# Moving two layer normalisations and a residual add into the loop of a feed-forward on one Trainium2 core

## What is computed

```python
x = x + layernorm(differential_attention(layernorm(x)))      # stage a
x = x + layernorm(depth_2_block(layernorm(x)))                # stages n0, b0, f0, b1, f1, n1
x = x + layernorm(state_space(layernorm(x)))                  # stage s
x = x + layernorm(mixture_of_experts(layernorm(x)))           # stage mx

# depth_2_block, twice (l = 0, 1): local attention (stage b), then the feed-forward (stage f)
h = shift_token(x)                       # the upper 64 features come from the token before
h = (h - mean) / sqrt(var + 1e-5) * ln_g + ln_b
a, g = split(h @ w1 + b1)                # 128 -> 2 x 341
x = x + (a * gelu(g)) @ w2 + b2          # 341 -> 128
```

## Time and profile before

| | us |
|---|---|
| median of 3 runs (2048.04 to 2049.25) | 2048.75 |
| profiled execution | 2051.13 |
| its span, first to last instruction | 2049.3 |
| PE busy in the span | 1719.8 |
| DVE busy | 1544.9 |
| ACT busy | 1363.4 |
| POOL busy | 877.9 |
| second feed-forward, from its first transposes to the last residual add | 1608.9 to 1690.6 |
| separate stage, from its first statistics to its last application | 1691.9 to 1725.8 |
| state space, from its first transposes | from 1726.0 |

### The profile page before, as it was taken

One profiled execution on the slowest core, in us unless ns is written; L12 is line 12 of the kernel. 1 busy time (PEld: TensorE's weight loads), 2 busy tenths in 40 slices (PEclk: granted clock), 3 DMA queues, 4 the chain that ended last, 5 costly groups with the idle time before them and its releaser, 6 DMA issues. The chain is left out here.

```text
span 2049.3 us, 39274 instructions
## 1 busy us (share of the span) xinstructions
PE 1719.8 (84%) x12410; PEld 1128.4 (55%) x12410; DVE 1544.9 (75%) x4156; ACT 1363.4 (67%) x4708; POOL 877.9 (43%) x816
## 2 busy tenths in 40 slices
PE   4999999999999955999999695999999683753991
PEld 2555555555555532777777352777777351552660
DVE  2898889988889965899999365899998365663445
ACT  2888888888888862888888222888888226322555
POOL 3555655555655543233233123233233123285555
PEclk9999999999999976999999896999999896755995
DMA  7990000000000000000000100000000100012324
GB/s 205 185 184 11 2 1 2 1 2 1 2 2 2 2 1 6 12 17 12 16 17 12 32 19 6 11 17 13 16 16 13 32 19 1 6 45 66 84 64 133
DMA packets 102525, 65.90 MB, mean 32 GB/s; under 512 B 27698, under 2 KB 93874, under 8 KB 102322
## 3 DMA queue, kind: packets, MB, share of 16 engines
q1 hardware_dynamic: 97970, 54.40, 13.3%
q0 software_dynamic: 4352, 8.99, 1.3%
HBM read 19.50 MB, written 30.24 MB: 24 GB/s over the span
## 5 line engine op out<-in xcount | busy, mean ns | idle before, releaser
L411 ACT ACTIVATE a_E<-a_psS,a_nm 128x128 f32<-128x128 f32 (+1 forms) x1028 | 419.9, 429 | 32.2 <-DVE a_nm L245 30.2
L216 POOL TENSOR_SCALAR a_aT<-a_dT 128x384 f32<-128x384 f32 x256 | 309.1, 1208 | 299.8 <-PE a_psO L529 187.6
L245 DVE TENSOR_REDUCE a_nm<-a_psS 128x2 f32<-128x256 f32 (+1 forms) x514 | 259.9, 546 | 43.9 <-PE a_psS L496 43.4
L492 PE MATMUL a_psS<-a_kT,a_qm 32*128 32x128 f32 (+1 forms) x2064 | 240.6, 351 | 5.4 <-issue 3.4
L270 DVE SCALAR_TENSOR_TENSOR a_d<-a_E,a_cf 128x128 f32<-128x128 f32 (+1 forms) x512 | 219.4, 468 | 27.9 <-DVE a_cf L259 1.4
L411 ACT ACTIVATION_READ_ACCUMULATOR a_E<-a_psS,a_nm 128x1 f32 x1028 | 220.7, 215 | 0.0
L830 POOL TENSOR_TENSOR b0rn<-b0ss,minus_half 128x16 f32<-128x16 f32 x36 | 107.2, 2977 | 223.6 <-DVE b0ss L866 223.6
L830 POOL TENSOR_TENSOR b1rn<-b1ss,minus_half 128x16 f32<-128x16 f32 x36 | 107.2, 2977 | 223.0 <-DVE b1ss L866 223.0
L420 ACT ACTIVATE a_dT<-a_psT 128x384 f32<-128x384 f32 x256 | 127.0, 496 | 73.9 <-PE a_psT L505 71.2
L492 PEld LDWEIGHTS a_psS<-a_kT,a_qm 32*128 32x128 f32 x2064 | 136.6, 186 | 55.9 <-issue 35.6
L505 PE MATMUL a_psT<-ident,a_d 128*128 128x128 f32 x768 | 132.6, 282 | 6.8 <-DVE a_d L270 1.0
(11 more groups left out here) (353 smaller groups left out, 4424.1 us busy)
## 6 DMA issues: line engine op xcount, KB each, us to landing
mx_rows<-mx_blank SPq DMA_DIRECT2D x9, 2080.0 KB, 31.2
mx_xin<-mx_rows SPq DMA_DIRECT2D x72, 65.0 KB
b0v<-b0v SPq DMA_DIRECT2D x34, 128.0 KB, 2.3
b1v<-b1v SPq DMA_DIRECT2D x34, 128.0 KB
F<-mx_results SPq DMA_DIRECT2D x8, 256.0 KB, 5.2
mx_second<-mx_results SPq DMA_DIRECT2D x8, 256.0 KB, 5.4
out_dram<-X SPq DMA_DIRECT2D x8, 256.0 KB, 2.3
f0z<-F SPq DMA_DIRECT2D x9, 128.0 KB
```

The source lines that it names most:

```text
L216: pool.tensor_scalar(aT[:, s, :], dT[:, s, :], 0.0, None, ALU.max).then_inc(positived.sem, 1)
L245: ins = dve.tensor_reduce(nm[:, s, t, :], psS[:, s, :, (0, P)[t]:(P, 384)[t]], axis=AX.X, op=ALU.max, negate=True)
L411: ins = act.activation(E[:, s, m, c0:c1], psS[:, s, m, c0:c1], ACT.Exp, bias=nm[:, s, t, m:m + 1], accum_out=Z[:, p, h, t, m:m + 1])
L492: pe.matmul(psS[:, s, m, c0:c1], qm[rows, p, a, r, t * P:(t + 1) * P], kT[rows, p, a, 0:c1 - c0], start=(t == 0), stop=False)
```

## The change

`feed_forward` gets an optional argument `X`. With it (l = 1 only) the turn of group k also does pieces of the normalisations and of the residual for the groups behind it; three rounds of leftovers follow the loop. `add_normalised` and its call are deleted; `hand_on` and the empty block stay. The order of the pieces on the engines, in turn k:

- DVE: behind the variance, the shifts of inner group k-2 and outer group k-3; behind the gates, the statistics of inner group k-1 and outer group k-2; then the wait for psY and the residual add as before.
- ACT: the inner application of group k-2 ahead of the third gelu; the outer application of group k-3 behind the evacuation of the transposes.
- POOL: behind `fb`, the add X + F of group k-2 (on DVE before), the inner power of group k-1, the outer power of group k-2.

The diff, cut to its core (the deleted function is the one described above):

```diff
-def add_normalised(nc, name, X, F, minus_half):
...
-def feed_forward(nc, name, F, consts, w):
+def feed_forward(nc, name, F, consts, w, X=None):
...
+        BATCHES = 2 * PAIRS
+        if X is not None:
+            inner = Layernorms(nc, ctx, name + "i", F, minus_half)
+            outer = Layernorms(nc, ctx, name + "o", X, minus_half)
+            applied, summed = sem("applied"), sem("summed")
...
+        def normalised(g):
+            return X is not None and 0 <= g < BATCHES
...
+            def normalise_groups(k):
+                if normalised(k - 2):
+                    pool.wait_ge(applied, k - 1)
+                    xs = inner.tiles(X, k - 2)
+                    pool.tensor_tensor(xs, xs, inner.tiles(F, k - 2), ALU.add).then_inc(summed, 1)
+                if normalised(k - 1):
+                    inner.power(pool, k - 1)
+                if normalised(k - 2):
+                    outer.power(pool, k - 2)
...
                     pool.tensor_tensor(fb[:, :, :], f_of(pair, half), b2[:, :].unsqueeze(1).broadcast_to([P, NT, D]),
                                        ALU.add).then_inc(fb_ready.sem, 1)
+                    normalise_groups(2 * pair + half)
+            normalise_groups(BATCHES)
+            normalise_groups(BATCHES + 1)
...
+            def shifts(k):
+                if normalised(k - 2):
+                    inner.shifts(dve, k - 2)
+                if normalised(k - 3):
+                    outer.shifts(dve, k - 3)
+
+            def group_statistics(k):
+                if normalised(k - 1):
+                    dve.wait_ge(added.sem, added.at(0, 0, k))
+                    inner.statistics(dve, k - 1)
+                if normalised(k - 2):
+                    dve.wait_ge(summed, k - 1)
+                    outer.statistics(dve, k - 2)
...
                     variance(pair, half + 1)
+                    shifts(2 * pair + half)
                     for j, m in parts:
...
                             normalise(pair, half, 1)
+                    group_statistics(2 * pair + half)
                     dve.wait_ge(y_full.sem, y_full.at(pair, half, 1))
...
                     own.end()
+            for k in range(BATCHES, BATCHES + 3):
+                shifts(k)
+                group_statistics(k)
...
+            def inner_apply(k):
+                if normalised(k - 2):
+                    inner.apply(act, k - 2, inner.tiles(F, k - 2)).then_inc(applied, 1)
+
+            def outer_apply(k):
+                if normalised(k - 3):
+                    outer.apply(act, k - 3, outer.tiles(F, k - 3))
...
                     for j, m in parts:
+                        if j == J - 1:
+                            inner_apply(2 * pair + half)
                         act.wait_ge(g_full.sem, g_full.at(pair, half, j + 1))
...
                     take_x(x_full.at(pair, half, 1))
+                    outer_apply(2 * pair + half)
+            for k in range(BATCHES, BATCHES + 3):
+                inner_apply(k)
+                outer_apply(k)
...
-                feed_forward(nc, f"f{l}", F, consts, wF[l])
+                feed_forward(nc, f"f{l}", F, consts, wF[l], X if l == 1 else None)
...
-                add_normalised(nc, "n1", X, F, minus_half)
```

## The result

| | before | changed |
|---|---|---|
| median, us (4 runs each, side by side) | 2048.39 | 2033.53 |
| lowest to highest, us | 2046.78 to 2049.25 | 2032.36 to 2035.20 |
| profiled execution, us | 2051.13 | 2034.3 |
| its span, us | 2049.3 | 2032.5 |
| ratio of times | 1 | 0.9929 (95% interval 0.9916 to 0.9942) |

The change gains 14.9 us in the medians. Forecast were 14.2 us and 2034.5, with a range of 2025.5 to 2041.

A forecast was written before the change was run, and what follows sets the result against it. Bound by VectorE for part of each turn, TensorE otherwise, then a serial 36.11 us stage: 36.11 - 13.0 - 1.3 = 21.8 us gained, minus 7.6 for the port, is 14.2; 2048.75 becomes 2034.5 us, range 2025.5 to 2041.

The forecast's parts named there:

- What bounds it: Second feed-forward turn of 9.70 us: VectorE bounds from 1682.87 to 1686.95, TensorE the rest; the separate 36.11 us stage is serial.
- what the moved work costs: In the turns: moved applications, powers, statistics and shifts fit into waits and cost nothing; only the X+F add costs.
- The cover: VectorE's 3.04 us wait for the output product hides 2.80 us of statistics a turn, leaving 0.24 us.
- The tail: Leftovers behind the loop: a chain of 12.28 us plus nine handovers of 0.08, 13.0 us, replaces the 36.11 us stage.
- stage boundary: Between the leftovers and the state space: semaphore clearing and empty block stay, 1.28 us; lower bound 0.26.
- The port: Turns three on: POOL's X+F add holds the shared port, VectorE's remaining TENSOR_SCALARs stand 1.26 us, 7.6 us in six turns.
- (a): Rival: VectorE keeps the port through its four TENSOR_SCALARs or the add comes behind them; 2027.0 us, chance 0.20.
- Rival (b): The add gets in and the wider gap lowers TensorE's clock in one to three turns; 2036.5 to 2042 us, chance 0.18.
- The sum: Whole kernel: 21.8 us gained from the stage minus 7.6 us lost in the turns, a gain of 14.2 us.
- (c): Rival: TensorE's clock stays at the lower level from the third turn on; slower than before, 2071 us, chance 0.03.
- (d): Rival: the moved statistics overrun their hole on VectorE; 1 to 3 us more, 2035.5 to 2037.5 us, chance 0.07.
- (e): Rival: the tail stays long because some link serialises, by more boundary or ScalarE behind; 2038 to 2046 us, chance 0.04.

The follow-up runs named there:

- experiment 1: Changed kernel with one more wait: POOL's X+F add starts only behind VectorE's four TENSOR_SCALARs; 2025.33 us, ratio to before 0.9891.
- experiment 2: Changed kernel with the X+F add given back to VectorE, ahead of the outer statistics; 2026.65 us, ratio to before 0.9895.
- experiment 4: Changed kernel with POOL's X+F add of groups 0 to 5 replaced by a power of 128x4; 2025.88 us, one run.
- experiment 3: Changed kernel with POOL's bias add and X+F add behind the four TENSOR_SCALARs, in both feed-forwards; 2015.16 us, ratio to before 0.9830.
- experiment 6: Changed kernel with POOL doing the X+F add twice in each of six turns, first into a spare tile; 2046.78 us, one run.
- 9: Experiment 3 with reordered leftovers: group 7's inner power ahead of the X+F adds, its shift ahead of group 6's outer statistics; 2013.46 us, ratio to before 0.9828.
- 10: Kernel of 9 with one more wait: POOL's X+F add of group 6 starts only behind group 7's shift; 2010.13 us, ratio to before 0.9826.

## Why the prediction was right

**What bounds it, and what the moved work costs.** Right. The applications on ScalarE, the powers on POOL, and the statistics and shifts on VectorE are hidden (experiment 1: 9.69 us a turn with all of them inside). The cover for the 2.80 us of statistics is as tight as stated: 0.25 us are left, and 0.68 us more on VectorE stick out with 0.38 (experiment 2).

**The tail.** The chain of 13.0 us took 12.89 (1696.46 to 1709.35, where the last application ends). The stage boundary behind it took 1.75 us and not 1.28. The profiles show one of two values: 1.75 in all three of the changed kernel and in experiment 4, 1.30 to 1.32 in experiments 1, 2, 3, 6, 9 and 10, one profile each. What decides is open.

**The port.** The mechanism and the place were right: the X+F add comes directly behind the bias add and gets in after one TENSOR_SCALAR. Experiment 1 takes it away by order alone, 4 shows that the add and not a busy POOL does it, 6 adds a third one that stands. What the runs show is who stands beside whom; that the two engines share a port is the prediction's explanation of it, and no run looks inside. The ground on which (a) was held unlikely was also weaker than it read: the 1.12 us of the earlier trace rows are those of a power, and in experiment 4 a power and the TENSOR_SCALARs don't hold each other at all (1.02 and 2.03), so that row said little about an add. The mis-sized term is the price. I took the add's whole duration, 1.26, for each of six turns; it is 0.95. The TENSOR_SCALAR that stands begins 0.05 us after the add and finishes almost together with it, and the 0.26 us that it would have needed anyway (the last three of the four share 0.76 in the earlier trace rows) lie within the same time: 1.26 - 0.26 - 0.05, about 0.95. Experiment 6 gives 0.97 for the next one. So the term is 5.7 us and not 7.6. Nor was the add "stretched a little over 1.26", as I said the profile would show: it takes 1.257 to 1.267 in all eight cases.

**The clock.** Rival (b), to which I gave a chance of 0.18, took place beside the forecast's mechanism, once in each of the three profiles. The gap in front of the output product (1.24 + 0.66 us of waiting) cost 1.64 us in one turn of six; I had priced a fall at 2 to 2.9. With a gap wider by 0.96 it is four turns of six (experiment 6), with the gap of the kernel before none (experiment 1). By these runs the wider gap is needed for the fall, but it doesn't decide alone: five turns with the same gap kept the full clock.

**The sum.** 36.11 - 14.64 = 21.5 for the stage (21.8 forecast), 5.7 + 1.6 = 7.4 for the loop (7.6 forecast). The forecast of 14.2 met 14.1 by the profile because a term too large by 1.9 stood beside one of 1.6 that it left out. What was removed, what was hidden and what was not were right; that the sum came within a microsecond was partly luck. Rival (a), POOL not getting in between, would have read 2027.0 and is refuted; (c), a clock that stays low, too. The overrun of (d) isn't there, and of the longer tail of (e) only the 0.47 us of the boundary.

## What to carry to other kernels

When work moves between queues, ask not only whether each engine has time for it, but which operation of VectorE stands at the moment when GpSimd's add starts: an add of 512 elements a partition held the second of four TENSOR_SCALARs, and so the two behind it, for a microsecond, at a place where VectorE was the bound. POOL's result, done at 1647.25, was wanted only at 1650.48. One wait that lengthens nothing puts such an add beside operations that it doesn't hold; here it was worth 7.4 us in the loop of the changed kernel, and 10 more for an add that had always stood there. And where a gap on TensorE widens, look at the granted clock turn by turn, since the mean over a span hides one slow turn.

## What the runs showed of the hardware

- Beside an add of 128x512 on GpSimd, VectorE's TENSOR_SCALARs (SBUF to SBUF) and even a SCALAR_TENSOR_TENSOR of 128x4 with two operands in SBUF stand until it ends (1.28, 1.30, 1.22 us instead of 0.33 and 0.15). Gates with an operand in PSUM (0.75 us in the earlier trace rows) and statistics (0.86 for four in experiment 3, an aggregation in the earlier trace rows) run on.
- A power of 128x4 on GpSimd, 1.02 us long, holds no TENSOR_SCALAR (four TENSOR_SCALARs in 2.03 beside the bias add and the power, 2.02 to 2.04 beside the bias add alone). That differs from the Trainium skill's "SBUF — State Buffer", section "SBUF: two separate sides", by which any GpSimd operation holds the shared ports for its whole instruction; here the measurement decides. A power can itself be held: 1.45 us beside VectorE's add with two operands in SBUF.
- TensorE's granted clock fell to its lower level where it waited twice, 1.24 and 0.66 us, with 0.66 us of transposes between, always in the same one of six such turns; with 2.20 and 0.66 us in four of six; with 0.28 and 0.66 us it never did in this loop. The fall made a product of 2.94 us take 4.57.
- The boundary ahead of the state space took about 1.31 or 1.75 us behind the last application, 1.75 in three profiles out of three of the changed kernel; what decides is open.
